# A fused state-space and mixture-of-experts kernel: the expert tiles' Gelus in pairs, and another order of ScalarE's work in every second turn

## The reference

```python
# state-space branch
x_ssm, x_gate = split(xn @ W_in + b_in)
x_conv = silu(causal_depthwise_conv(x_ssm) + conv_b)
B, C = split(x_conv @ W_bc + b_bc);  dt = softplus(x_conv @ W_dt + b_dt)
h = h * exp(dt * A) + (dt * x_conv) * B        # a recurrence over time, 16 states
y = sum_n(h * C) + x_conv * D
branch1 = layernorm((y * silu(x_gate)) @ W_out + b_out + xn)
# expert branch: 8 experts, the best 2 of each token
h = gelu(layernorm(xn @ w1[e] + b1[e]) * ln1_g[e] + ln1_b[e])
branch2 = layernorm(sum over the 2 experts of weight * (h @ w2[e] + b2[e]) + xn)
```

## Time and profile before

| | |
|---|---|
| median of 3 runs | 1819.2 us (1811.06 to 1820.54) |
| the profiled execution's own time | 1810.14 us |
| its span, first to last instruction | 1808.1 us |
| busy, share of the span | PE 86%, DVE 85%, ACT 81%, POOL 56% |
| mean granted TensorE clock | 0.959 of full speed |

### The profile page before, as it was taken

One profiled execution on the slowest core, in us unless ns is written; L12 is line 12 of the kernel. 1 busy time (PEld: TensorE's weight loads), 2 busy tenths in 40 slices (PEclk: granted clock), 3 DMA queues, 4 the chain that ended last, 5 costly groups with the idle time before them and its releaser, 6 DMA issues.

```text
span 1808.1 us, 28219 instructions
## 1 busy us (share of the span) xinstructions
PE 1546.5 (86%) x6882; PEld 941.6 (52%) x6882; DVE 1534.0 (85%) x2498; ACT 1458.1 (81%) x2552; POOL 1009.1 (56%) x594
## 2 busy tenths in 40 slices
PE   5988379898988998989899888989888998886588
PEld 4655145555555565555555555555555655554232
DVE  5766488999999999999898989999999999931797
ACT  3554279898989889898989898989889898966587
POOL 2777756655655656555655556556556565532233
PEclk9777789999999999999999999999999999999799
DMA  7999643333334333333333433333333333322995
GB/s 234 351 294 377 238 119 84 95 97 99 95 84 112 84 95 90 100 90 100 83 103 86 109 84 102 98 92 98 89 103 84 94 97 95 88 45 48 284 293 175
DMA packets 183269, 234.43 MB, mean 130 GB/s; under 512 B 46527, under 2 KB 148936, under 8 KB 183131
## 3 DMA queue, kind: packets, MB, share of 16 engines
q1 hardware_dynamic: 141646, 171.58, 30.9%
q0 software_dynamic: 26160, 36.06, 10.7%
q10 hardware_dynamic: 15328, 25.20, 4.0%
HBM read 149.07 MB, written 83.70 MB: 129 GB/s over the span
## 4 chain that ended last, share of the span: by engine, by line
DVE 40%; ACT 26%; issue 14%; PE 13%; ACTq 3%; POOL 2%; DMA 1%; DVEq 0%; SPq 0%; POOLq 0%
DVE area L1285 8%; DVE area L1298 5%; ACT area L667 4%; DVE area L1315 4%; DVE area L1294 4%; ACT psD L661 3%; DVE more L1347 3%; ACT L706 3%; ACT h_T L701 3%; ACT L709 3%; PE psT L1030 3%; PE psX L982 3%; DVE h_norm L1328 2%; DVE more L1344 2%; ACTq L688 2%
## 5 line engine op out<-in xcount | busy, mean ns | idle before, releaser
L543 POOL TENSOR_TENSOR area<-area,more 128x1024 f32<-128x1024 f32 x258 | 604.4, 2360 | 547.5 <-DVE area L1298 276.3
L1315 DVE TENSOR_TENSOR area<-area,psD 128x1024 f32<-128x1024 f32 x256 | 310.0, 1211 | 0.3 <-issue 0.2
L972 PE MATMUL psH<-w_sb,ffn_xT 128*128 x544 | 265.0, 610 | 5.8 <-ACT ffn_xT L677 5.7
L520 POOL DMA_INDIRECT expert_d<-y_out,meta x139 | 219.6, 1580 | 78.4 <-ACT y_out L683 49.6
L982 PE MATMUL psX<-w_sb,h_T 128*128 x1088 | 261.6, 383 | 0.8 <-ACT y_out L683 0.8
L1003 PE MATMUL psY<-ident,area 128*128 128x128 f32 x2048 | 250.7, 276 | 0.0
L982 PEld LDWEIGHTS psX<-w_sb,h_T 128*128 128x128 f32 x1088 | 202.4, 190 | 59.4 <-issue 32.5
L667 ACT ACTIVATE area<-area,A_sb 128x512 f32<-128x512 f32 x258 | 171.5, 712 | 76.5 <-DVE area L1298 41.4
L1003 PEld LDWEIGHTS psY<-ident,area 128*128 128x128 f32 x2048 | 222.2, 141 | 13.4
L701 ACT ACTIVATE h_T<-psT,be_T,g_T 128x128 f32<-128x128 f32 x540 | 202.2, 460 | 4.5 <-PE psT L962 4.5
L661 ACT ACTIVATE psD<-area,A_sb 128x512 f32<-128x512 f32 x258 | 177.9, 690 | 33.9 <-DVE area L1285 14.5
(11 more groups left out here) (187 smaller groups left out, 2492.2 us busy)
## 6 DMA issues: line engine op xcount, KB each, us to landing
more<-B_rows_d SPq DMA_DIRECT2D x130, 512.0 KB, 3.9
xin<-sorted_x SPq DMA_DIRECT2D x137, 128.0 KB, 2.1
more<-ssm_d SPq DMA_DIRECT2D x18, 512.0 KB, 3.9
area<-xnT_d SPq DMA_DIRECT2D x17, 512.0 KB, 3.6
mamba_d<-mo_stage SPq DMA_DIRECT2D x17, 512.0 KB, 2.9
area<-L_attn_x SPq DMA_DIRECT2D x8, 1024.0 KB, 6.8
xnT_d<-w_sb ACTq DMA_DIRECT2D x16, 512.0 KB, 6.8
expert_d<-area ACTq DMA_DIRECT2D x8, 1024.0 KB
```

The lines of the kernel that those rows point to most:

```text
L543: pool.tensor_tensor(inflow[:, k], dtx, B_rep[par][:, k].rearrange("p (a t) -> p a t", a=1).to_broadcast([P, KD, CHUNK]), ALU.mult).then_i ...
L972: nc.tensor.matmul(psH[:, :], ffn_xT[:, k, :], w1_sb[:, bass.ds(e, 1), k, :].rearrange("p o h -> p (o h)"), start=(k == 0), stop=False)
L1315: V.tensor_tensor(h, h, C_rep[k].rearrange("p (a t) -> p a t", a=1) .to_broadcast([P, KD, CHUNK]), ALU.mult).then_inc(S[f"hC{k}_done"], 1)
```

## The change

The Gelus of two tiles, u-1 and u, are computed together in every even turn, between one load of Gelu's table and one of Exp's. Odd turns have no Gelus. psT holds one tile's transposes at a time, so in an even turn PE transposes tile u between the two groups of Gelus; the transposes of an odd turn's tile stand at the end of that turn. In odd turns ACT does `hidden_root` and `copy_xT` first, then the decays, `copy_y`, and the take at the end. Both Silus share one table load, in turn 1. `down` and the scatter of a tile come one turn later, so there are two buffers of normed rows and three of Gelu's output. `up` stands ahead of `transpose_h`, and the even turns' `task` behind `add_up`. `bc_middle` moves from turn 4 to 6, `bc_residue` from 3 to 4 and `bc_lowest` from 5 to 7. The expert numbers are read where they are used, and start-up dummies for the semaphores go.

```diff
-LAG = 2
+LAG = 3
...
+        h_T2 = scan_area.take(KH, P)
+        h_norm2 = scan_area.take(HIDDEN)
...
+        h_norms = [h_norm[:, :], h_norm2]
+        h_Ts = [h_T[:, 0], h_T[:, 1], h_T2]
...
+                        if u > LAG:
+                            y_at_hand(u - 1 - LAG)
...
+                if t > LAG:
+                    act.wait_ge(S["y_ready"], t - LAG)
...
+                e = expert(u)
+                act.wait_ge(S["hT_done"], u + 1)
+                if u >= 3:
+                    act.wait_ge(S["y_ready"], u - 2)
...
-                        e, e_y = expert(u), expert(u - LAG)
-                        decay0_of(u + 1, 0, state[0], g, par)
-                        decay1_of(u + 1, state[1], par)
-                        hidden_root(u)
-                        if pr == 0:
-                            take("gate1", c, half)
-                        elif pr == TASKS.index("out0") + 1:
-                            take_out(c, 0, psT[:, :])
-                        elif pr == TASKS.index("out1") + 1:
-                            take_out(c, 1, psT[:, :])
-                        elif TASKS[pr - 1] is not None:
-                            take(TASKS[pr - 1], g, ahead)
-                        decay0_of(u + 1, 1, state[0], g, par)
-                        copy_xT(u + 1)
-                        if pr == 0:
-                            copy_sum(c)
-                        if pr == BC_TAKEN + 1:
+                        if pr % 2 == 1:
+                            hidden_root(u)
+                            copy_xT(u + 1)
+                            decay0_of(u + 1, 0, state[0], g, par)
+                            decay1_of(u + 1, state[1], par)
+                            decay0_of(u + 1, 1, state[0], g, par)
+                            if u >= LAG:
+                                copy_y(u - LAG)
+                            if TASKS[pr - 1] is not None:
+                                take(TASKS[pr - 1], g, ahead)
+                        else:
+                            decay0_of(u + 1, 0, state[0], g, par)
+                            decay1_of(u + 1, state[1], par)
+                            hidden_root(u)
+                            if pr == 0:
+                                take("gate1", c, half)
+                            elif pr == TASKS.index("out0") + 1:
+                                take_out(c, 0, psT[:, :])
+                            elif pr == TASKS.index("out1") + 1:
+                                take_out(c, 1, psT[:, :])
+                            else:
+                                take(TASKS[pr - 1], g, ahead)
+                            decay0_of(u + 1, 1, state[0], g, par)
+                            copy_xT(u + 1)
+                            if u >= LAG:
+                                copy_y(u - LAG)
+                            if pr == 0:
+                                copy_sum(c)
+                        if pr == BC_TAKEN + 3:
                             bc_middle(g, ahead)
                         if pr == DT_TAKEN:
                             soft_exp(g)
                             soft_ln(g)
-                        with_gelu()
-                        copy_y(u, (pr - LAG) % RING, pr % 2, e_y)
-                        gelu(u, pr % 2, e)
+                        if pr % 2 == 0:
+                            with_gelu()
+                            if u > 0:
+                                gelu(u - 1)
+                            gelu(u)
+                            with_exp()
                         if pr == CONV_TURN:
+                            gate_silu_of(c, half)
                             act.wait_ge(S["seed_done"], g + 1)
                             conv_silu(g)
-                        if pr == GATE_TURN:
-                            gate_silu_of(c, half)
-                        with_exp()
+                            with_exp()
...
+                pe.wait_ge(S["norm_done"], u + 1)
+                if u > 0:
+                    pe.wait_ge(S["gelu_done"], u)
                 for k in range(KH):
-                    m = nc.tensor.transpose(psT[:, k * P:(k + 1) * P], h_norm[:, k * P:(k + 1) * P], ident[:, :])
+                    m = nc.tensor.transpose(psT[:, k * P:(k + 1) * P], h_norms[u % 2][:, k * P:(k + 1) * P], ident[:, :])
...
-                        e_down, e_up = expert(u - 1), expert(u + 1)
-                        if pr == 0:
-                            wait_taken("gate1", c)
-                        elif TASKS[pr - 1] is not None:
-                            wait_taken(TASKS[pr - 1], g)
-                        transpose_h(u)
-                        up(u + 1, e_up)
+                        if u == 0:
+                            wait_taken("gate1", 0)
+                            transpose_h(0)
+                        up(u + 1)
                         spread_C0(u + 1, state[0], par, g)
-                        early_C = pr not in (CONV_TURN - 1, CONV_TURN, DT_TAKEN + 1)
-                        if early_C:
+                        if pr % 2 == 0:
+                            if u > 0:
+                                transpose_h(u)
                             transpose_x(u + 2)
-                            spread_C1(u + 1, state[1], par)
-                        if pr == 0:
-                            transpose_sum(c)
+                            if pr == 0:
+                                transpose_sum(c)
+                            early_C = pr not in (CONV_TURN - 1, DT_TAKEN + 1)
+                            if early_C:
+                                spread_C1(u + 1, state[1], par)
+                            if u >= 2:
+                                down(u - 2)
+                            if not early_C:
+                                spread_C1(u + 1, state[1], par)
+                            if pr == 0:
+                                seed(c)
+                            add_up(u, pr % 2)
+                            if TASKS[pr] is not None:
+                                pe.wait_ge(S["gelu_done"], u + 1)
+                                task(TASKS[pr], g)
                         else:
-                            pe.wait_ge(S["gelu_done"], u + 1 + 1)
-                        if pr == TASKS.index("out0"):
-                            project_out(c, 0, psT[:, :])
-                        elif pr == TASKS.index("out1"):
-                            project_out(c, 1, psT[:, :])
-                        elif TASKS[pr] is not None:
-                            task(TASKS[pr], g)
-                        if not early_C:
-                            transpose_x(u + 2)
-                            spread_C1(u + 1, state[1], par)
-                        down(u - 1, (pr + 1) % 2, e_down)
-                        if pr == 0:
-                            seed(c)
-                        add_up(u, pr % 2)
-            wait_taken("gate1", CHUNKS)
+                            early_C = pr != CONV_TURN
+                            if early_C:
+                                transpose_x(u + 2)
+                                spread_C1(u + 1, state[1], par)
+                            pe.wait_ge(S["gelu_done"], u)
+                            if TASKS[pr - 1] is not None:
+                                wait_taken(TASKS[pr - 1], g)
+                            if pr == TASKS.index("out0"):
+                                project_out(c, 0, psT[:, :])
+                            elif pr == TASKS.index("out1"):
+                                project_out(c, 1, psT[:, :])
+                            else:
+                                task(TASKS[pr], g)
+                            if not early_C:
+                                transpose_x(u + 2)
+                                spread_C1(u + 1, state[1], par)
+                            if u >= 2:
+                                down(u - 2)
+                            add_up(u, pr % 2)
+                            wait_taken(TASKS[pr], g)
+                            transpose_h(u)
...
             for u in range(MAMBA_TURNS, FFN_TURNS):
-                e_down, e_up = expert(u - 1), expert(u + 1)
+                up(u + 1)
                 transpose_h(u)
-                up(u + 1, e_up)
                 if u == MAMBA_TURNS:
                     for j in range(2):
                         project_out(CHUNKS, j, psY[:, j * CHUNK:(j + 1) * CHUNK])
                 transpose_x(u + 2)
-                down(u - 1, (u - 1) % 2, e_down)
-            down(FFN_TURNS - 1, (FFN_TURNS - 1) % 2, expert(FFN_TURNS - 1))
+                down(u - 2)
...
-                dve.wait_ge(S["hT_done"], u + 1)
-                V.tensor_scalar(h_norm[:, :], psH[:, :], hmv[:, 0:1], hrs[:, 0:1], ALU.subtract, ALU.mult
+                if u >= 2:
+                    dve.wait_ge(S["hT_done"], u - 1)
+                V.tensor_scalar(h_norms[u % 2], psH[:, :], hmv[:, 0:1], hrs[:, 0:1], ALU.subtract, ALU.mult
...
-                        if pr == BC_TAKEN:
```

(7 more changed lines are left out.)

94 lines of the change are left out of this document (44 added, 50 removed).

## The result

The changed kernel takes 1803.19 us (median of 11 runs, 1796.14 to 1812.03); the kernel before, on the same chip, 1816.6 us (11 runs, 1811.06 to 1824.94). The ratio is 0.9915, 95% interval 0.9894 to 0.9936: 0.85% faster, where 2.8% was forecast, and above the range's 1800. The profiled execution took 1804.77 us, its span 1803.0.

What follows compares the result with a forecast made beforehand. DVE sets the pace, held up by ACT's late root: 1810.1 - 73.5 (root waits) + 16 (new waits) + 7.5 (tail) = 1760 us profiled, 1764 us as median; range 1742 to 1800.

Steps and rivals of the forecast that it cites:

- The failed step: DVE's work at turn ends in the loop: bc_residue costed at 0.6 us, finish_dt at 2.4 us.
- ACT's relief: ACT in the loop: 10 table loads a chunk instead of 18, so 76.4 us a chunk down to 66.1.
- The waits for the root: DVE's norm waiting for ACT's root in the loop: 73.5 us go; the new trace should show 10 to 20.
- New waits of 16 us: DVE in the loop: 0.4 for add_up and 0.25 + 0.1 + 0.3 for the root, 1.0 us a chunk.
- the layout: Loop turns laid out step by step on ACT, PE and DVE; root 0.25 us late in turn 4, add_up's slack 0.4.
- The reads at nothing: PE's two reads of expert numbers a turn, about 0.30 us each, stay hidden behind add_up or up: zero cost.
- the very sign that the prediction named for it: PE's up or down idle 0.3 us or more with everything they wait for done, meaning the reads are exposed.
- slower: Rival: PE's reads in the loop no longer covered, about 1855 us; chance 0.11.
- PE as the bound: Rival: PE becomes the loop's bound, its 80.8 us a chunk growing to 83.5; about 1785 us, chance 0.16.
- the rival's 1785: Total time if PE becomes the loop's bound: about 1785 us; chance 0.16.
- The tail: Seven turns with a tile alone, behind the loop: 7.4 us each against 6.8, +4; with one later tile +7.5 together.
- the one more tile: Behind the last Gelu, one more tile to be weighted and scattered: 3 us, at most one whole turn, 6.8.

Runs made afterwards that it cites:

- e1: Changed kernel with bc_residue, bc_lowest and finish_dt moved from a turn's end to between two scans, away from GpSimd's multiply; 1785.75 us, ratio 0.9836.
- e10: e1 with the edits of e4, e5 and e6 added; 1770.59 us, ratio 0.9747 to the kernel before.
- e4: Changed kernel with turn 7's second spread of C and transpose_x put behind the projection; 1804.44 us, ratio 0.9937.
- e5: e1 with both of PE's reads of expert numbers at the turn's start, ahead of up; ratio 0.9763 to the kernel before.
- e6: Changed kernel with transpose_h ahead of up again in the seven turns with a tile alone; ratio 0.9898 to the kernel before.
- e12: e10 with the first convolution between turn 0's scans and the second, with its padding, ahead of turn 1's scan1; ratio 1.0071 to the kernel before.
- e2: Changed kernel with DVE waiting for GpSimd's multiplies ahead of bc_residue, bc_lowest and finish_dt in their old place; 1821.68 us, ratio 1.0035.

## Why the prediction was wrong, point by point

**The failed step** is the one that gave DVE's work the lengths that it had before: "bc_residue (0.6, estimated from the 0.80 of the norm)" and "finish_dt's 2.4 us". These, like the 682 and 1219 ns of the trace, were lengths of operations that a root wait of up to 2.0 us had pushed behind GpSimd's multiply. With the wait gone they take 1.57 and 2.08 us (the first of `finish_dt`'s two). Measured in the engine: +39.0 us where the sum had 0; e1 and e10 show it by undoing it. The trace of before held a sign: a convolution's first operation was in the collision there already, at 1.29 us in the mean (L1344).

The profiled execution was to take 1760 and took 1804.8. The gap of 45 us: DVE's longer operations 39.0; the tail 12.6 instead of 7.5, 5.1; ahead of the loop and behind the last `down` 2.6; the idle time in the loop fell by 59.3 instead of 57.5, -1.8. Without the collision the time is inside the range: e1 takes 1785.75.

- *ACT's relief: right.* 160 table loads in the loop are 10 a chunk, and 1057.2 us over 16 chunks are 66.1, the forecast's number.
- *The waits for the root: right, even too cautious.* 73.5 became 2.1, where 10 to 20 were left in the forecast.
- *New waits of 16 us: right in sum, but by luck, since not in place.* The root's 2.1, 6.1 for `add_up`, and 9.0 in the loop for the gate, which the layout didn't have, are 17.2. Why the gate's came isn't settled: without PE's stop in turn 7 they are 0.8 (e4), but 0.4 in e1 too, where that stop stays.
- *The reads at nothing: wrong, and small.* PE was idle for them 16.8 us, 0.38 in the mean and up to 0.6, the very sign that the prediction named for it; moving them gave 4.0 us of loop in e5. The rival "slower" needed them on the path each time. The lead of PE's sequencer seen at 880.0 doesn't reach the read ahead of `down`.
- *PE as the bound: right as the next bound.* In the changed kernel DVE hid it; in e1, without the collision, 29.8 us of waits for `add_up` appear. A forecast of 1760 could hardly have been met even without the collision: e1's span is 1780.7 us and that of e10, with reads and tail edited too, 1762.6 (its runs' median is 1770.59). That the rival's 1785 is e1's time is in part chance, since its prices were others.
- *The tail: mechanism right, sizes off.* 7.4 us a turn were forecast and 7.75 measured; one turn took 9.35 and one 9.02, as their `up` took 3.19 and 2.56 us instead of 1.98. The first `up` to the last is 56.6 us where the kernel before has 50.2 for its transposes: 6.4 where the sum had 4. From there to the end of the last `down` it is 14.0 instead of 8.0 us: 6.0 where the sum had 3 for the one more tile. Of three stops of PE of the same 2.7 us only the second was followed by a slow `up` (start, duration on PE after):

```profile
1623.39 1.98 PE L996 MATMUL psH<-w_sb,ffn_xT 128*128 x4 [2.71 <-DVE area L1368]
...
1631.14 3.19 PE L996 MATMUL psH<-w_sb,ffn_xT 128*128 x4 [2.71 <-DVE h_norm L1368]
...
1640.49 1.98 PE L996 MATMUL psH<-w_sb,ffn_xT 128*128 x4 [2.72 <-DVE area L1368]
```

  The granted clock from 1631.1 to 1634.4 was 0.60, and 1.00 around the other two. e10's turns take 6.83 us (1595.47 to 1602.30), the 6.8 of the earlier trace rows: of the 0.92 less than 7.75, 0.47 were `up`'s place (e6) and 0.45 the reads, which cost nothing as long as `up` stood first (e5's turns take 7.76). Even so e10 spends 71.2 us there against before's 63.9: 3.0 more ahead of the first transposes, where a pair's Gelus must end, a term that the sum didn't have, and 4.3 more at the end, where it had 3.

Left open: what share of e1's and e10's remaining 20 to 30 us of waiting for `add_up` could be had by reordering PE's list; why a turn alone took 7.75 us and not 7.4; and what the exposed reads cost in all. No run tried the first, none settles the others.

## What to carry to other kernels

The duration of an instruction in a trace holds for its neighbours in time. Before a stall is costed as gained, list what runs *behind* the stalled instruction and what another engine does at that moment without the stall; for a DVE operation with two SBUF operands or a TENSOR_SCALAR from SBUF to SBUF, look for GpSimd's reads. And before an operation is moved out of a collision, see which instruction it then delays and what is queued behind that one: here 0.76 us saved on DVE cost 3 to 5 us through ACT's list.

## What the runs showed of the hardware

- DVE's operations with both operands in SBUF are held by GpSimd's multiply: one that takes 0.68 us alone ended 0.55 after it, one of 1.22 ended 1.08 after it, and GpSimd's multiply isn't slowed (2359 and 2362 ns). A TENSOR_SCALAR from SBUF to SBUF is held too: in the changed kernel 1.47 us from 1503.76, 0.28 beyond the end of a multiply at 1504.95, and 0.53 alone (e12). The norm, a TENSOR_SCALAR that reads PSUM, isn't: 805 to 807 ns beside the same multiply.
- Waiting for GpSimd by a semaphore cost more than being held: 48.4 us of waits against 41.7 of lengthening (e2).
- In the changed kernel a stop of PE of 1.60 us was followed by 2 us at a granted clock of 0.50, the 1.2 GHz level, in which four matmuls of a projection took 3.35 us instead of 1.88 (403.43). The loop's mean clock was 1.00 before, 0.97 in the changed kernel and 0.99 in e10. In the tail, stops of 2.7 us were followed by such a stretch in some turns only.
